# The second block's MLP beside the first block's attention of the sequence two ahead, and its attention half beside the first block's MLP

## The reference

```python
# block 0: quantized ("bitlinear"), 16 heads
xn = rmsnorm(x, g1) * (1 + scale) + shift
qkv = act_quant(xn) @ weight_quant(w_qkv).T + b
x = x + bitlinear(softmax(q k^T / sqrt(32)) v, w_proj)
x = x + bitlinear(gelu(bitlinear(adaln(x), w_fc1)), w_fc2)     # 512 -> 2048 -> 512
# block 1: fp32, one head of width 512
h = film(rmsnorm(x, w)); s = (h q_w)(h k_w)^T / sqrt(512)
x = x + softmax(s) (h v_w) proj_w
x = x + gelu(film(rmsnorm(x)) mlp_w1) mlp_w2
```

## Time and profile before

| | us |
|---|---|
| median of 3 runs | 2240.01 |
| lowest, highest | 2236.99, 2245.3 |
| span of the profiled execution | 2237.3 |

### The profile page before, as it was taken

The page is one execution under the profiler, slowest core; times in us unless marked ns, Lnnn a source line. Parts: engine busy times, 40 slices in busy tenths (PEclk is TensorE's granted clock), DMA queues, the critical chain, the costliest instruction groups (busy, mean ns, idle before and its releaser), DMA issues.

```text
span 2237.3 us, 40636 instructions
## 1 busy us (share of the span) xinstructions
PE 1987.5 (89%) x13326; PEld 1003.8 (45%) x13503; DVE 1530.2 (68%) x2667; ACT 1144.3 (51%) x2090; POOL 772.1 (35%) x705
## 2 busy tenths in 40 slices
PE   4787878899989998899989998899989998899889
PEld 3354334544444444544444444544444444544434
DVE  5676657875688657875688757875788757875422
ACT  4575644754465543844466443844456443744230
POOL 2173433641255113640255113740255103741021
PEclk8899999999999999999999999999999999999989
DMA  8443533021311123031411123021321123021212
GB/s 303 144 172 109 201 127 99 26 104 62 129 49 58 67 96 99 26 104 62 128 49 58 67 96 99 26 104 53 118 68 53 72 96 99 26 71 44 94 38 94
DMA packets 85529, 200.87 MB, mean 90 GB/s; under 512 B 7612, under 2 KB 48864, under 8 KB 73144
## 3 DMA queue, kind: packets, MB, share of 16 engines
q1 hardware_dynamic: 77528, 174.88, 23.4%
q10 hardware_dynamic: 7776, 23.10, 2.8%
HBM read 161.97 MB, written 35.72 MB: 88 GB/s over the span
## 4 chain that ended last, share of the span: by engine, by line
PE 42%; issue 28%; POOL 17%; DVE 7%; ACT 5%; DMA 0%; POOLq 0%; ACTq 0%; SPq 0%; DVEq 0%
POOL memory L1257 12%; PE banks L1435 8%; PE banks L1434 8%; PE banks L1436 8%; PE banks L1327 5%; PE banks L1392 5%; DVE memory L1012 2%; PE banks L1309 1%; POOL memory L1004 1%; PE banks L1378 1%; POOL memory L1180 1%; ACT memory L1045 1%; POOL memory L1474 1%; DVE memory L1019 1%; DVE memory L1027 1%
## 5 line engine op out<-in xcount | busy, mean ns | idle before, releaser
L1435 PE MATMUL banks<-memory 128*128 128x512 bf16 x1512 | 574.2, 380 | 19.5 <-DVE memory L1506 6.6
L1434 PE MATMUL banks<-memory 128*128 128x512 bf16 x1438 | 550.4, 383 | 23.1 <-DVE memory L1559 7.8
L1436 PE MATMUL banks<-memory 128*128 128x512 bf16 x1491 | 566.4, 380 | 1.3
L1257 POOL TENSOR_TENSOR memory<-memory 128x512 bf16<-128x512 f32 x332 | 375.7, 1152 | 366.5 <-ACT memory L1246 365.2
L1246 ACT ACTIVATE memory<-banks 128x512 f32<-128x512 f32 x512 | 290.9, 599 | 129.6 <-PE banks L1239 127.2
L1660 POOL TENSOR_TENSOR memory<-memory 128x512 bf16<-128x512 f32 x128 | 144.7, 1132 | 487.6 <-DVE memory L1655 487.6
L1189 PE MATMUL banks<-memory 96*128 96x512 bf16 x512 | 186.7, 392 | 73.6 <-DVE memory L1201 39.1
L1434 PEld LDWEIGHTS banks<-memory 128*128 128x128 bf16 x1536 | 149.0, 97 | 217.1 <-issue 15.5
L1201 DVE TENSOR_REDUCE memory<-banks 128x1 f32<-128x512 f32 x320 | 207.8, 680 | 37.6 <-PE banks L1189 37.4
L1436 PEld LDWEIGHTS banks<-memory 128*128 128x128 bf16 x1536 | 148.5, 97 | 186.7 <-issue 4.3
L1435 PEld LDWEIGHTS banks<-memory 128*128 128x128 bf16 x1536 | 152.1, 99 | 165.4 <-issue 3.8
(11 more groups left out here) (176 smaller groups left out, 2951.2 us busy)
## 6 DMA issues: line engine op xcount, KB each, us to landing
memory<-weight_parts SPq DMA_DIRECT2D x80, 1024.0 KB, 4.9
memory<-head_parts SPq DMA_DIRECT2D x192, 128.0 KB, 2.8
head_parts<-memory SPq DMA_DIRECT2D x64, 256.0 KB, 2.8
memory<-in_x SPq DMA_DIRECT2D x32, 256.0 KB, 3.3
memory<-ada_rows SPq DMA_DIRECT2D x16, 512.0 KB, 4.5
memory<-in_L_cond_w_fc ACTq DMA_DIRECT2D x2, 4096.0 KB, 14.3
memory<-in_L_cond_mlp_w SPq DMA_DIRECT2D x8, 1024.0 KB, 7.7
weight_parts<-memory SPq DMA_DIRECT2D x8, 1024.0 KB, 4.9
```

Of the source, the lines that this page charges most:

```text
L1257: eng.tensor_tensor(prob_lo[:, e % RING], expo[:, e % RING], prob_hi[:, e % RING], ALU.subtract).then_inc(ok.sem, 1)
L1434: pe.matmul(bank, lh, rh, start=(k == 0), stop=False)
L1435: pe.matmul(bank, lh, rl, start=False, stop=False)
L1436: mm = pe.matmul(bank, ll, rh, start=False, stop=(k == KC - 1))
```

## The change

Work is in three stages instead of two. Each engine's list becomes `opening()` (block 0 of sequence 0), `attention(i, j, k)` and `rest(i, j)`. `attention` has block 0's first norm to its slots for sequence i, the MLP of block 1 for k = i - 2, and, near its end, the first norm and FiLM of block 1 for j = i - 1. `rest` has block 0's projection and MLP for i beside the attention half of block 1 for j. Ten products of `M` go ahead of the slots, 18 go into 72 slots as quarters (three matmuls each), four come behind. The lists run `attention(1, 0, None)`, `rest(1, 0)`, six times both with i from 2 to 7, then `attention(None, 7, 6)`, `rest(None, 7)`, `attention(None, None, 7)`.

```diff
+M_FRONT, M_SLOTS, M_JOBS = 10, 18, 32
+PARTS = ((0,), (1,), (2,), (3,))
+FIRST_SLOTS = HEADS + LEAD
+QUARTERS = [s if s < FIRST_SLOTS else FIRST_SLOTS + (s - FIRST_SLOTS) * 4 // 3 for s in range(4 * M_SLOTS)]
+for s, at in enumerate(QUARTERS):
+    M_AT.setdefault(slot(at), []).append((M_FRONT + s // 4, PARTS[s % 4]))
+ACT_M_AT, DVE_M_AT, POOL_M_AT = after_job(1), after_job(2), after_job(3)
+HAND_AT = {(0, 12): 0, (0, 14): 1, (0, 16): 2, (0, 18): 3}
+NORM_AT = {(4, 1): 0, (4, 4): 1, (4, 7): 2, (4, 10): 3}
...
# squares0: block 0's first squares are written to y, and wait no more for the hand-over
-                    if j is not None:
-                        act.wait_ge(handed.sem, handed(j, t + 1))
-                    act.activation(x0[:, t], x_next[:, t], ACT.Square, scale=float(D) ** -0.5,
+                    act.activation(y[:, t], x_next[:, t], ACT.Square, scale=float(D) ** -0.5,
...
# block 1's norms and FiLMs are all ACT's; the first norm reads x1 and writes normed1
-            dve.tensor_scalar(wide[:, c % 2], banks[:, b], film_now[:, 0, c:c + 1],
-                              film_now[:, 1, c:c + 1], ALU.mult, ALU.add).then_inc(free[b].sem, 1)
+            act.activation((normed1, y1)[a][:, t], x1[:, t], ACT.Copy, scale=rstd1[:, a, t:t + 1]
+                           ).then_inc(y1_ok.sem, 1)
+            act.activation(wide[:, c % 2], banks[:, b], ACT.Identity, scale=film_now[:, 2 * a, c:c + 1],
+                           bias=film_now[:, 2 * a + 1, c:c + 1]).then_inc(free[b].sem, 1)
...
# SP
+            def attention(i, j, k):
+                units(k, 4, 6)
...
+                    for c in range(2):
+                        spill_parts(sp, i, c)
+                        stack_parts(sp, i, c)
...
# ACT, attention
+                    act.wait_ge(sq1.sem, sq1(j, TT))
+                    squares0(act, i, 0)
+                gelus(k, range(0, 5))
+                    round0(act, i, 0)
...
+                for c, n in slots():
+                        head_slot(i, c, n)
+                    if (c, n) in ACT_M_AT:
+                        gelus(k, (ACT_M_AT[c, n],))
...
# ACT, rest (i's and j's steps in this order)
+                    round0(act, i, 2)
+                qv_high(act, j, 1, 0)
+                qv_high(act, j, 1, 1)
+                    copy_xq(act, i, 2)
+                qv_high(act, j, 1, 2)
+                    gelu0(act, i, 0)
+                qv_high(act, j, 1, 3)
+                    round_hidden(act, i, 0)
+                exp_1(act, j, 0)
+                exp_1(act, j, 1)
...
+                exp_1(act, j, 2)
+                    gelu0(act, i, 1)
+                exp_1(act, j, 3)
+                    round_hidden(act, i, 1)
+                p_high(act, j, 2)
+                p_high(act, j, 3)
...
+                    copy_hidden(act, i, 2, (0, 1))
+                    norm1(act, j, 1, t)
+                    gelu0(act, i, 3)
+                    copy_hidden(act, i, 2, (2, 3))
+                film_full(act, j, 1, 0)
+                film_high(act, j, 1, 0)
+                film_full(act, j, 1, 1)
+                film_high(act, j, 1, 1)
+                    round_hidden(act, i, 3)
...
# DVE, rest
+                    amax0(dve, i, 2)
+                    scales0(dve, i, 2, 2)
+                qv_low(dve, j, 1, 0)
+                qv_low(dve, j, 1, 1)
+                    whole0(dve, i, 2)
+                qv_low(dve, j, 1, 2)
+                    hidden0(dve, i, 0)
+                    hidden_scales(dve, i, 0)
+                qv_low(dve, j, 1, 3)
+                r_sum(dve, j)
...
+                    block0_out(dve, i, 0)
+                    whole_hidden(dve, i, 1)
+                p_low(dve, j, 2)
...
# PE, attention
+                products(k, range(0, 6))
+                    turn_xq(pe, i, 0)
+                    spread_scales(pe, i)
+                products(k, range(6, 7))
+                    qk_product(pe, i, 0)
...
+                for c, n in slots():
+                    for m, ks in M_AT.get((c, n), []):
+                        products(k, (m,), ks)
+                        head_slot(i, c, n)
+                products(k, range(last, last + 1))
+                    last_heads(i)
+                    turn_y1(pe, j, 0, i)
+                products(k, range(last + 1, M_JOBS))
# PE, rest
+                    turn_xq(pe, i, 1)
+                q1(pe, j, 0)
+                    proj0(pe, i)
+                for c in range(1, KC):
+                    q1(pe, j, c)
+                for t in range(2):
+                    v1(pe, j, t)
+                    turn_xq(pe, i, 2)
+                v1(pe, j, 2)
+                    fc1_0(pe, i, 0)
+                v1(pe, j, 3)
+                r_1(pe, j)
+                s1(pe, j, 0)
+                s1(pe, j, 1)
+                turn_p1(pe, j, 0)
...
+                s1(pe, j, 3)
+                    fc2_0(pe, i, 0)
+                turn_p1(pe, j, 2)
+                turn_p1(pe, j, 3)
+                proj1(pe, j, 0)
...
+                proj1(pe, j, 3)
+                    turn_hidden(pe, i, 2, (0, 1))
+                    fc1_0(pe, i, 3)
+                    turn_hidden(pe, i, 2, (2, 3))
+                turn_y1(pe, j, 1)
+                    fc2_0(pe, i, 2)
+                    turn_hidden(pe, i, 3, range(4))
+                    fc2_0(pe, i, 3)
```

More of the change, by code:

```diff
@@ L1887, in join, with gelus, ramp @@
-            def join(j, place):
-                for step in JOIN_ACT.get(place, ()) if j is None else ():
+            def gelus(k, jobs):
+                if k is not None:
+                    for m in jobs:
+                        if M[m][0] == "fc1":
+                            gelu_1(act, k, *M[m][1:])
+            def ramp(steps):
+                for name, w, *n in steps:
+                    if name == "abs":
+                        magnitudes(act, w, *n)
+                    elif name == "read":
+                        read_late(act, w, *n)
+                    elif name == "weight":
+                        read_weight_act(act, *weight_turns[w][1:], *n)
+                    elif name == "store":
+                        store_ada(act, 1)
+                    elif w == "fc1":
+                        load_ternary(act, "fc1")
+                    elif w == "fc2":
+                        act.wait_ge(prep["rows_out"], 32)
+                        load_ternary(act, "fc2")
+                    elif w == "plain":
+                        load_plain(act)
@@ L1889, in join @@
+            def join(place):
+                for step in JOIN_ACT.get(place, ()):
                     name, _, n = step.partition(" ")
@@ L2040, in join @@
+            def join(place):
+                for step in JOIN_DVE.get(place, ()):
                     name, _, n = step.partition(" ")
@@ new lines, in rest @@
+                p_low(dve, j, 2)
+                p_low(dve, j, 3)
+                for t in range(2):
+                    invert1(dve, j, t)
+                    proj_add1(dve, j, t)
+                    if i is not None and t == 0:
+                        hidden0(dve, i, 2)
+                        hidden_scales(dve, i, 2)
+                if i is not None:
+                    block0_out(dve, i, 1)
+                    whole_hidden(dve, i, 2)
+                for t in range(2, TT):
+                    invert1(dve, j, t)
+                    proj_add1(dve, j, t)
@@ L2250, in both, with ramp @@
-            def both(i, j):
-                products1(j, Q + V[0:2])
+            def ramp(steps):
+                for name, w, *n in steps:
+                    if name == "total":
+                        total(pe, w)
+                    elif name == "turn":
+                        turn_late(pe, w, *n)
+                    elif name == "emb":
+                        condition(pe, w, n)
+                    elif name == "film":
+                        turn_film(pe, w)
+                    elif name == "weight":
+                        turn_weight(pe, *weight_turns[w], *n)
@@ new lines, in last_heads, with opening @@
+            def last_heads(i):
+                for (c, _), h in VALUES_AT.items():
+                    if c > KC:
+                        weigh_values(pe, i, h)
+            def opening():
+                turn_xq(pe, 0, 0)
+                spread_scales(pe, 0)
+                qk_product(pe, 0, 0)
+                qk_product(pe, 0, 1)
+                v_product(pe, 0)
+                for c, n in slots():
+                    late_product(0, c, n)
+                    ramp(RAMP_PE.get((c, n), []))
+                    head_slot(0, c, n)
+                last_heads(0)
+                join("proj")
+                no_turn_pe(pe)
+                turn_xq(pe, 0, 1)
+                proj0(pe, 0)
+                join("gain")
+                join("turn")
+                turn_xq(pe, 0, 2)
+                fc1_0(pe, 0, 0)
+                join(0)
+                fc1_0(pe, 0, 1)
+                for t in range(1, TT + 1):
```

(6 more changed lines are left out.)

948 lines of the change are left out of this document (494 added, 454 removed).

## The result

The changed kernel takes 2481.32 us (median of 4 runs, 2478.21 to 2489.15) against 2241.29 for the kernel before, run beside it: 1.1079 times as long, 95% interval [1.1052, 1.1107]. Forecast were 2375 us and a range of 2265 to 2450. So the direction was right, and the time lay 106 us above the forecast and 31 us above the range.

The account below looks back on a forecast made before the run. TensorE was taken as the bound, with 224 us of work and 29 idle in a 252.8 us period. Opening 306, first period 127 + 106, six periods of 266 (1596), tail 84 + 67 + 89 sum to 2375 us; range 2265 to 2450.

Parts of the forecast that it names:

- Direction: Whole kernel: slower than before, chance 0.88.
- the pipeline's price: Outside the six periods: 779 us against 720 for the same pieces before, so the deeper pipeline costs 59 us.
- Table loads: Exp and Gelu alternate: 16 loads a period for 2; in the key slots they stop TensorE 6 to 7 us.
- Key slots: Slots with the exponentials, five gelus set between them: 78 us (62.6 before), idle 7; bounds 73 and 90.
- The waits of the last stretch: Block 0's MLP beside block 1's attention: TensorE idle 25 us, including 6.3 before turning chunk 2 and 4.0 at proj1(0).
- Head: Period's start up to block 0's first score: 40 us (53.1 before), with a wait of about 4.5.
- query slots: Score slots that only go by query: 24.5 us (29.0 before), 23 on TensorE against some 20 on DVE.
- the last stretch taken as 81 us of work and 25 us of waits: Block 0's MLP beside block 1's attention: 106 us (87.9 before), bounds 88 and 118.
- Worse: Rival: idle stretches drop the clock, up to 5 us a period, slipping exponentials another 8; period 279, 2453 us; chance 0.08.
- Mild loss: Rival: last stretch's mid waits vanish, table loads mostly hide; period 250 to 254, 2279 to 2303 us; chance 0.20.
- gain: Rival: quarters fill the slots' idle time, last stretch near its 81 us of work; period 238, 2185 us; chance 0.09.

Follow-up runs that it names:

- the version with all three causes away: Changed kernel with the fastest order, unused products in TensorE's waits, and Tanh for the second block's Gelu (another output): 2339.60 us, 1.0455.
- the fastest order: The first reordering plus VectorE's gain and shift two tiles at a time and V's last copy ahead of the scales: 2400.61 us, 1.0736.
- the first reordering: Changed kernel with V's copies before rounding, V's third product before turning chunk 2, probability splits before hidden tile 1's round and subtraction: 2418.44 us, 1.0813.
- the further moves: The first reordering plus gain and shift by two tiles, V's last copy before scales, tile 2's down projection before turning y1: 2440.20 us, 1.0887.

## Where the forecast was right, and where it failed

- **Direction and the pipeline's price: right.** Outside the six periods there are 787 us (779 forecast), against 719 for the same pieces before: a price of 68 us (59 forecast). The opening and first attention with their last stretches came out at 548.4 (539 by the sum), the tail at 239 (240). The point from which the change would pay was given as 243 us a period. With 776 us outside, as in the version with all three causes away, it is (2237 - 776)/6 = 243.5; that version has 259.5.
- **Table loads: right.** Sixteen a period, as counted. 6 to 7 us of exposed load in the key slots were forecast; taking them away brought 8.5. Key slots 78 forecast, 79.0 measured.
- **The waits of the last stretch: right in place and sum** (25 forecast, 24.3 measured). It is the written order that makes them: moving a few lines (the fastest order) took 8 us of them away (22.2 to 14.0 booked), while the work of the engines stayed.
- **Head and query slots: 4.6 and 2.0 us too low.** In the head the forecast had one wait of 4.5 us and about 1 at the first score. In its place two Gelus are late (3.0), two turnings wait 1.9, and the first score waits 1.5 for the DMA of the stacked heads; with 0.2 more, and 0.16 for each of the six, that is 7.6. A mean clock of 0.96 adds 1.8. The 34.6 us of work were right within about 1.
- **The step that failed: the last stretch taken as 81 us of work and 25 us of waits, 106 in all.** Both terms were right, but the sum took every matmul at the full rate, behind each wait too. The clock was named only in the rival *Worse*, as up to 5 us a period. It measures 27.9 us a period at the half clock, which is 14 of the 283.3; 11.4 of them in the last stretch, where the miss is 10.3. Over six periods that is 84 of the 104 us by which they missed, and over the whole span (1 - 0.937) x 2487 = 157 us against (1 - 0.978) x 2237 = 49 before, in full-rate time: 108 of the 250 us by which the span grew, if all of it reached the path. The row that could have told it was shown: the lone attention half at 0.89 with 52 of 67 us busy. I read it as a matter of one idle part, and took for the last stretch, which I forecast with 25 us idle in 106, that of a stretch with 2.5 us idle in 88.
- **The rivals.** *Mild loss* and *gain* fall: the waits did not vanish, and a period never came below 255 us. *Worse* names the right cause, and 279 a period is near the 283.3, but 8 of its 13 us stood on slipping exponentials, which did not slip. With the clock at its measured price the forecast's own sum is 2375 + 6 x 14 = 2459; the other 28 us are the head, the query slots and the first period's last stretch (115.6 for 106).

## What to carry to other kernels

When a change puts waits of 2 to 5 us into a stretch of TensorE that had next to none, price them at one and a half to two times their length: once as waits, and again for the clock behind them. In the last stretch here 24 us of waits came with 11 us of clock; the first reordering brought 5 us of waits and 5.7 of clock. The factor is a reading of this kernel, and the sum of the waits alone does not fix it (the further moves). Ask of each function that needs a table load not how long the load is but who waits behind it: the same load cost nothing measurable beside long products and 0.85 us among exponentials with two banks between ACT and TensorE. And before a step is moved ahead of a wait, look up what the moved step itself waits for.

## What was not expected of the hardware

- One program, one execution: identical waits and identical work of the other engines, but the last stretch takes 116.7 us in one period and 113.5 in another, by the granted clock alone (0.90 and 0.92). The whole periods take 286.9 and 279.8 us, at 0.94 and 0.96, of which 0.7 us are longer waits in the head. What decided between them in a given period no run here shows.
- A stretch at a booked 81% of TensorE (94 of 117 us) has a mean clock of 0.90; the 0.89 of before belonged to 78%.
- DVE's `gain0` slows down when POOL's bias addition (L1014) works on other tiles of the same tensor: 14 of its 64 instructions, with that addition beside them from start to end, take 1.58 us, and the other 50 take 0.75 (the four tiles of a chunk are one line here, of the changed kernel's last stretch).
```profile
1581.74 4.40 DVE L1022 SCALAR_TENSOR_TENSOR memory<-memory 128x512 f32<-128x512 f32 x4
```
